# Attention scores of one head as three accumulating 32-row products in the four row quarters, with the shift as the exponential's bias

## What is computed

```python
q = (layernorm(x) @ Wq + bq).reshape(B, L, 16, 32)
k = (ctx @ Wk + bk).reshape(B, S, 16, 32)
v = (ctx @ Wv + bv).reshape(B, S, 16, 32)
scores = jnp.einsum('blhe,bshe->bhls', q, k)
A = jax.nn.softmax(scores / sqrt(32), axis=-1)
out = jnp.einsum('bhls,bshd->blhd', A, v)
x = x + out.reshape(B, L, 512) @ Wo + bo
x = x + routed_experts(layernorm(x))
```

## Time and profile before

| what | value |
|---|---|
| three runs | 2516.39, 2518.48, 2520.16 us |
| profiled execution, span from first to last instruction | 2509.0 us |
| profiled execution, its own time | not listed apart; the runs' median is 9.5 us above its span |
| TensorE, VectorE, ScalarE, GpSimd busy | 96%, 86%, 73%, 16% of the span |
| stages | projections to about 289 us, attention to about 2057, then output projection, routing, experts |

### The profile page before, as it was taken

The page is one execution under the profiler, slowest core; times in us unless marked ns, Lnnn a source line. Parts: engine busy times, 40 slices in busy tenths (PEclk is TensorE's granted clock), DMA queues, the critical chain, the costliest instruction groups (busy, mean ns, idle before and its releaser), DMA issues. The chain is left out here.

```text
span 2509.0 us, 36972 instructions
## 1 busy us (share of the span) xinstructions
PE 2419.7 (96%) x13522; PEld 1284.1 (51%) x13522; DVE 2152.2 (86%) x1941; ACT 1839.9 (73%) x2157; POOL 402.6 (16%) x512
## 2 busy tenths in 40 slices
PE   8999679999999999999999999999999999969998
PEld 7878434444444444444444444444444447758776
DVE  4368479999999999999999999999999998867555
ACT  3123368998988899899899988989889975634332
POOL 2113200100000000000000000000000003225665
PEclk9999789999999999999999999999999999979999
DMA  7436790011142001104100111510110107734473
GB/s 270 157 130 218 192 213 22 23 22 27 26 111 51 22 23 27 27 22 122 40 22 23 27 27 29 128 27 23 24 30 22 31 25 266 235 110 144 131 224 121
DMA packets 131353, 214.12 MB, mean 85 GB/s; under 512 B 26823, under 2 KB 64167, under 8 KB 130413
## 3 DMA queue, kind: packets, MB, share of 16 engines
q1 hardware_dynamic: 104268, 144.67, 20.7%
q0 software_dynamic: 24576, 59.52, 7.8%
q10 hardware_dynamic: 2336, 7.60, 0.9%
HBM read 146.36 MB, written 83.04 MB: 91 GB/s over the span
## 5 line engine op out<-in xcount | busy, mean ns | idle before, releaser
L1118 ACT ACTIVATE probs<-psum 128x1024 f32<-128x1024 f32 x1600 | 1508.9, 1035 | 149.8 <-PE psum L1269 145.7
L1269 PE MATMUL psum<-q_st,k_st 97*128 97x512 f32 x3200 | 922.9, 419 | 32.5 <-ACT probs L1118 17.5
L1269 PEld LDWEIGHTS psum<-q_st,k_st 97*128 97x128 f32 x3200 | 548.8, 189 | 609.7 <-ACT probs L1118 413.7
L1181 DVE TENSOR_TENSOR even_sums<-even_sums,probs 128x2048 f32<-128x2048 f32 x352 | 804.6, 2286 | 16.9 <-ACT probs L1118 16.9
L1290 PE MATMUL psum<-probs,v_st 128*32 128x512 f32 x6400 | 800.0, 601 | 0.0
L1181 DVE TENSOR_TENSOR odd_sums<-odd_sums,probs 128x2048 f32<-128x2048 f32 x320 | 731.4, 2285 | 1.0
L1290 PEld LDWEIGHTS psum<-probs,v_st 128*32 128x32 f32 x6400 | 152.3, 108 | 352.2 <-issue 263.9
L2050 PE MATMUL psum<-we_hi,wo 128*128 x624 | 216.7, 408 | 5.3 <-DVE wo L1941 3.1
L798 POOL DMA_DIRECT2D sum_scratch<-shared_rows x31 | 18.3, 590 | 1212.8 <-ACT shared_rows L1076 1212.8
L1882 ACT ACTIVATE shared_rows<-hold 128x512 f32<-128x512 f32 x78 | 63.6, 815 | 103.2 <-DMA hold<-token_rows,whole 62.9
L2050 PEld LDWEIGHTS psum<-we_hi,wo 128*128 128x128 f32 x624 | 118.1, 189 | 32.7 <-issue 7.5
(11 more groups left out here) (230 smaller groups left out, 2030.3 us busy)
## 6 DMA issues: line engine op xcount, KB each, us to landing
q_st<-qh_scratch SPq DMA_DIRECT2D x64, 256.0 KB
k_st<-kh_scratch SPq DMA_DIRECT2D x56, 192.0 KB, 3.8
token_rows<-rows SPq DMA_DIRECT2D x8, 1028.0 KB, 6.7
xn<-in_x SPq DMA_DIRECT2D x16, 512.0 KB, 6.8
qh_scratch<-o_hi SPq DMA_DIRECT2D x8, 1024.0 KB, 4.5
ql_scratch<-o_lo SPq DMA_DIRECT2D x8, 1024.0 KB, 7.6
q_st<-ql_scratch SPq DMA_DIRECT2D x32, 256.0 KB
token_rows<-in_x SPq DMA_DIRECT2D x1, 8192.0 KB, 38.9
```

Of the source, the lines that this page charges most:

```text
L1118: nc.scalar.activation(probs[:, p_slot(it, t), 2 * half:2 * half + 2, :], psum[:, 2 * slot:2 * slot + 2, :], ACT.Exp, scale=SCALE).then_in ...
L1181: nc.vector.tensor_tensor(into[:], a, probs[:, p_slot(it, t)], ALU.add).then_inc(added, 1)
L1269: mm = nc.tensor.matmul(psum[:, 2 * slot + h % 2, :], k_st[:, h, t * P:(t + 1) * P], q_st[b][:, h, :], start=True, stop=True)
```

## The change

- `k_st` and `q_st` hold each head's 32 rows once, in the head's own row quarter (rows 32h to 32h+31), with high and low parts beside each other. Keys and queries come in two transfers instead of three, each over all 128 partitions.
- A head's scores of a tile are three matmuls of 32 rows that accumulate in its PSUM bank. They are issued term by term, the four heads of a term in the four row quarters and in four banks.
- Both pairs of a tile are issued together behind one wait, two tiles ahead of the weighing (`AHEAD_TILES`); `LEAD` and `burst_end` go.
- The shift is no longer in the product: each exponential takes `neg_bound` as a per-partition bias. The spread over 128 rows, its copy, its store and its load go; the root is scaled, and the norms are turned and repeated by a matmul with the identity.
- For wide inputs (`unbounded`) the bias is 0 and a second unrolled program with a fourth product carries each query's shift; TensorE and SyncE branch to one of two programs.
- The rest pair has three products over 128 rows, in which each head's two keys lie in its own rows. Fills of one row of ones go; `shift_ones`, `rest_shift` and a part of each `q_st` are filled by VectorE.

```diff
-LEAD = 7
+AHEAD_TILES = 2
+SHIFT_PART = 2
+TERMS = ((0, 0), (0, 1), (1, 0))
...
-                sp.wait_ge(neg_rows_ready, 1)
-                sp.dma_start(shift_d.rearrange("g j (c n) -> (g j c) n", n=CH), neg_rows.bitcast(F32)).then_inc(shift_stored, 16)
-
-                sp.wait_ge(shift_stored, 16)
-                load_shift(sp, g, 0, 0, g["q_in"][0])
...
-                act.activation(bound[:], widest[:], ACT.Sqrt, scale=SLACK).then_inc(bound_ready, 1)
-                act.wait_ge(neg_spread, 1)
-                act.activation(neg_rows, psum[:, Q_SUM_BANK, :], ACT.Copy).then_inc(neg_rows_ready, 1)
+                act.activation(bound[:], widest[:], ACT.Sqrt, scale=SCALE ** 2 * SLACK).then_inc(bound_ready, 1)
...
-                pe.transpose(psum[0:1, K_SUM_BANK, 0:P], norms[:], ident[:]).then_inc(norms_turned, 1)
-                pe.wait_ge(neg_ready, 1)
-                pe.matmul(psum[:, Q_SUM_BANK, :], ones_row[:], neg_bound[:], start=True, stop=True).then_inc(neg_spread, 1)
+                pe.matmul(psum[:, K_SUM_BANK, 0:P], norms[:].to_broadcast([P, P]), ident[:], start=True, stop=True).then_inc(norms_turned, 1)
...
 def load_queries(sp, g, b, it, count):
-    for r, src in enumerate((g["qh_d"], g["ql_d"], g["qh_d"])):
-        sp.dma_start(g["q_st"][b][r * DH:(r + 1) * DH, :, :].bitcast(F32),
-                     src.rearrange("(h d) j l -> d h (j l)", d=DH)[:, :, ds(it * CH, CH)]).then_inc(count, 16)
+    for part, src in enumerate((g["qh_d"], g["ql_d"])):
+        sp.dma_start(g["q_st"][b][:, part, :].bitcast(F32), src.rearrange("p j l -> p (j l)")[:, ds(it * CH, CH)]).then_inc(count, 16)
...
-        k_st = sb("k_st", [SH + 1, HG, S], F32R)
-        q_st = [q[0:SH + 1] for q in g["q_st"]]
+        k_st = sb("k_st", [P, 2, S], F32R)
+        q_st = g["q_st"]
...
-            for r, src in enumerate((kh_d, kh_d, kl_d)):
-                sp.dma_start(k_st[r * DH:(r + 1) * DH, :, first:first + n].bitcast(F32),
-                             src[:, ds(j, 1), first:first + n].rearrange("(h d) o s -> d (h o) s", d=DH)).then_inc(count, 16)
+            for part, src in enumerate((kh_d, kl_d)):
+                sp.dma_start(k_st[:, part:part + 1, first:first + n].bitcast(F32), src[:, ds(j, 1), first:first + n]).then_inc(count, 16)
...
                         nc.scalar.activation(probs[:, p_slot(it, t), 2 * half:2 * half + 2, :],
-                                             psum[:, 2 * slot:2 * slot + 2, :], ACT.Exp, scale=SCALE).then_inc(exp_done, 1)
+                                             psum[:, 2 * slot:2 * slot + 2, :], ACT.Exp, bias=neg_bound[:], scale=SCALE).then_inc(exp_done, 1)
...
-                fill_rows(dve, (HG // 2, HG), filled)
+                dve.memset(shift_ones[:].bitcast(F32), 1.0).then_inc(filled, 1)
+                for b in range(2):
+                    dve.memset(q_st[b][:, SHIFT_PART, :].bitcast(F32), 0.0).then_inc(filled, 1)
+                dve.memset(rest_shift[:].bitcast(F32), 0.0).then_inc(filled, 1)
...
+                def products(bank, h, b, t, term, start, stop):
+
+                    part, of = TERMS[term]
+                    rows = slice(h * DH, (h + 1) * DH)
+                    return nc.tensor.matmul(psum[:, bank, :], k_st[rows, part, t * P:(t + 1) * P], q_st[b][rows, of, :], start=start, stop=stop)
+
+                def scores(it, t, shifted):
+
+                    b, n = it % 2, place(t, 0)
...
+                    if it * NP + n + 1 >= S_RING:
+                        pe.wait_ge(exp_done, it * NP + n + 2 - S_RING)
+                    for term in range(len(TERMS)):
+                        last = term == len(TERMS) - 1 and not shifted
+                        for h in range(HG):
+                            bank = 2 * ((n + h // 2) % S_RING) + h % 2
+                            mm = products(bank, h, b, t, term, term == 0, last)
+                            if last and h % 2:
+                                mm.then_inc(s_ready, 1)
...
+                def step(it, shifted):
+
+                    for t in range(NT):
+                        if it == 0 and t == 0:
+                            for u in range(AHEAD_TILES):
+                                ahead(0, u, shifted)
+                        ahead(it, t + AHEAD_TILES, shifted)
+                        if t == REST_AT:
+                            weigh_rest(it)
+                        weigh(it, t)
...
+                    for it in range(NIT):
+                        step(it, True)
+                with pe.Else():
+                    for it in range(NIT):
+                        step(it, False)
```

More of the change, by code:

```diff
@@ L936, in piece_end, with queries_in @@
             return S if n == K_PIECES - 1 else sum(pieces[n]) * P
-        def fill_rows(eng, heads, count):
-            for n, (a, m) in enumerate(pieces):
-                eng.memset(k_st[SH:SH + 1, heads[0]:heads[1], a * P:piece_end(n)].bitcast(F32), 1.0).then_inc(count, 1)
+        def queries_in(it, shifted):
+            per = 48 if shifted else 32
+            return per * (it // 2 + 1) - (16 if shifted and it % 2 == 0 else 0)
         with nc.Block() as block:
@@ L1011, in result @@
                     store_result(sp, results, j, c)
-                def step(it):
+                def step(it, shifted):
                     j, c = divmod(it, NC)
@@ L1056, in _ @@
+                with sp.Else():
+                    weighted(False)
                 sp.wait_ge(s_ready, NIT * NP)
@@ new lines, in rest_scores @@
+                def rest_scores(it, shifted):
+                    b, bank = it % 2, 2 * (REST_PAIR % S_RING)
+                    pe.wait_ge(exp_done, it * NP + REST_PAIR + 1 - S_RING)
+                    if it % NC == 0:
+                        pe.wait_ge(added, it * adds + REST_KEYS_AT + 1)
+                    for term, (part, of) in enumerate(TERMS):
+                        mm = nc.tensor.matmul(psum[0:REST_ROWS, bank, :], rest_k[:, part, 0:REST_ROWS], q_st[b][:, of, :],
+                                              start=term == 0, stop=term == len(TERMS) - 1 and not shifted)
+                    if shifted:
+                        mm = nc.tensor.matmul(psum[0:REST_ROWS, bank, :], rest_shift[:, 0:REST_ROWS], q_st[b][:, SHIFT_PART, :], start=False, stop=True)
@@ L1336, in step @@
                             sum_even(it - 1)
-                for it in range(NIT):
-                    step(it)
+                pe.wait_ge(filled, FILLS)
+                with pe.If(pe.value_load(unbounded[0:1, 0:1], min_val=0, max_val=1) == 1):
+                    with pe.Fori(0, NG) as j:
+                        with pe.Fori(0, NC) as c:
+                            it = j * NC + c
+                            pe.wait_ge(ma_k_in, (j + 1) * 32)
+                            pe.wait_ge(ma_q_in, (it + 1) * 32)
+                            k = 0
+                            for t in range(TPC):
+                                for h in range(HG):
+                                    rows = slice(h * DH, (h + 1) * DH)
+                                    for half in range(2):
+                                        if k >= 2:
+                                            pe.wait_ge(ma_max, it * (TPC * HG * 2) + (k - 1))
+                                        elif k == 0:
+                                            pe.wait_ge(ma_max, it * (TPC * HG * 2))
+                                        k += 1
+                                        for b in range(4 * half, min(4 * half + 4, -(-S // CH))):
+                                            w = min(CH, S - b * CH)
+                                            for term, (part, of) in enumerate(TERMS):
+                                                mm = pe.matmul(psum[:, b, 0:w], q_st[0][rows, of, t * P:(t + 1) * P],
+                                                               k_st[rows, part, b * CH:b * CH + w], start=term == 0, stop=term == len(TERMS) - 1)
+                                        mm.then_inc(ma_mm, 1)
+                    pe.wait_ge(ma_q_in, (NIT * 2 + 3) * 16)
+                    for it in range(NIT):
[3 more added lines that the diff above has]
+                        step(it, False)
                 pe.wait_ge(wo_lo_ready, 2)
```

245 lines of the change are left out of this document (103 added, 142 removed).

## The result

The changed kernel takes 2755.99 us (median) against 2517.55 us for the kernel before beside it: **1.0946 times as long, interval 1.0928 to 1.0963.** The direction was forecast; the size was not: 2593 us was the forecast, 2535 to 2705 its range. Of its four timed executions three lie between 2754.57 and 2756.49 us; one took 5458.58 us and stands outside the ratio.

The account below looks back on a forecast made before the run. PE's own work was taken as the bound, DVE 2 us behind. Profiled span 2509 + 87 (32 iterations, each 2.7 us longer) - 12 at the start = 2584 us; with 9.5 us from span to median, forecast 2593, range 2535 to 2705.

Parts of the forecast that it names:

- What bounds the kernel now: Attention in the kernel before: PE's own work takes 53.4 of 54.46 us an iteration, DVE needs 52.4.
- ACT's step of 1.00 us: From one exponential to the next on ACT: 0.91 us becomes 1.00, some 52 us an iteration with small copies, still hidden.
- A group of four row quarters at 0.23 us: Score matmuls on PE: four heads' 32-row matmuls side by side take 0.23 us a group, 0.89 us a tile's scores.
- dear groups: Rival for the score matmuls: groups of four cost 0.30 us each, ring 2.30 us, 2700 us in all; chance 0.15.
- serial weight loads: Rival for the score matmuls: twelve weight loads follow one another, ring 2.63 us, 2971 us in all; chance 0.09.
- The ring of 2.16 us a tile: Exponential and scores wait for each other with nothing in reserve: 0.05 + 0.96 + 0.03 + 1.12 = 2.16 us a tile.
- The bias at 0.09 us: Per-partition bias on each exponential on ACT: 0.09 us longer, 1.03 to 1.12 us.
- The start at -12 us: Start of attention: first key load 3.3 us earlier and 9.0 us from less data ahead of Wo, together -12 us.
- The copy of O sits in the first of these gaps and costs nothing: In the sum for an iteration: ACT's copy of O falls in the gap at the first sum over keys, costing nothing.
- The clock rival: Rival for PE's clock: it falls to half, 120 us more for every tenth of the iterations; chance 0.04.
- The chance of 0.87 for slower: Whole kernel: slower by over 0.2% (5 us) was given 0.87, within that 0.04, faster 0.09.
- The signs: Trace marks of being right: rest-pair exponentials 57 us apart, exponentials near 1.12 us, DVE near 91%, Wo's split near 318 us.

Follow-up runs that it names:

- grain_f3: Kernel before, 97-row products and no bias, with both pairs of a tile behind one wait, two tiles ahead, and O copied before the fourth exponential: 2565.59 us, 1.0192.
- before_bias: Kernel before with a per-partition bias of zero added to every exponential of attention: 2571.58 us, 1.0222.
- fetch3_swap: fetch3 with the two waits ahead of a tile's scores exchanged, exponential first, then key piece: 2599.22 us, 1.0329.
- fetch3: Changed kernel with the copy of O moved from before the seventh exponential of an iteration to before the fourth: 2614.14 us, 1.0398.
- fetch3_nobias: fetch3 with the bias of the exponentials left out, so the shift is not applied: 2544.53 us, 1.0118.
- rows_pairs: Changed kernel with scores issued pair by pair, each with its own wait, in the old bursts: 2644.69 us, 1.0513.
- fetch5: Changed kernel with the copy of O one exponential earlier, before the sixth: 2699.72 us, 1.0735.
- grain_f6: grain_f3 with the copy of O back before the seventh exponential: 2669.72 us, 1.0627.
- wide_forced: Changed kernel with the test for wide inputs made to fail and the search loops unrolled: 8216.92 us, measured once.

## Why the prediction was right and wrong

- **What bounds the kernel now: right for PE, incomplete for ACT.** PE's own work was put at 53.4 us with DVE behind it; grain_f3 was summed from the same rows and came out within 0.3 us. But before_bias shows that ACT had no room to spare: 0.09 us more on each exponential made an iteration 1.69 us longer, where I had expected 1.0 at most, and where the prediction called ACT's step of 1.00 us "still hidden".
- **A group of four row quarters at 0.23 us: right.** The twelve matmuls and the switch take 0.90 us (985.72 - 984.82 in fetch3_swap), 0.89 was summed; they start in three groups of four, 0.33 and 0.23 us apart, the four of a group within 0.02 us. The way there was in part luck: the row it was read from shows a group of four side by side every 0.43 us in the weighing (four under way from 989.96, the next four from 990.41), and that such a matmul is two passes of 0.215 was assumed, not read. By the figure of 3.07 times in the Trainium skill (TensorE: Matmul & The Clock Gate, Measured speedup vs the span model), which I had held against the row, a group would cost an estimated 0.30 and these scores 1.03 us; the trace does not agree with it for this kernel. The rivals of dear groups and of serial weight loads fall with the same rows; the second was also summed too high, since its 1.43 and an exponential of 1.12 make a ring of 2.55 and not 2.63.
- **The ring of 2.16 us a tile: right**, 2.17 in the trace. In the unhindered form, fetch3_swap, an iteration is 57.59 us for 57.2 summed. Missed here: 0.10 us where a tile has two waits, 0.6 us an iteration. The remaining 0.4 was not traced.
- **The bias at 0.09 us: right**, 1.024 to 1.113 us, and in the ring with its full length.
- **The start at -12 us: right** in sum. Wo's split began at 319.07 us instead of 330.24, 11.2 us earlier (forecast near 318). The single terms shifted: SP's jump over the long program cost more than my 1.5 us. In the trace SP's branch ends at 285.23 and the first key load goes out 2.85 us later, at 288.08; in the kernel before these were 290.03 and 290.15. So the first key load is 2.1 us earlier, not 3.3, and less data ahead of Wo gave the rest:

```profile
284.35 1.28 ACT L1052 ACT_TABLE_LOAD   x1 [4.34 <-PEq L252]
...
288.08 0.33 SPq L889 DMA_DIRECT2D k_st<-kh_scratch  x1
...
319.07 1.91 ACT L1081 ACTIVATE wo<-even_sums 128x2048 fp32r<-128x2048 f32 x1 [2.35 <-DMA even_sums<-in_Wo]
```

- **The step that failed** stands in the list of an iteration: "The copy of O sits in the first of these gaps and costs nothing". I had asked what the copy does to ACT, and not who waits for it. The weighing of tile 0 does, and in the new order the scores of tile 3 are queued behind it. Put at nothing, it costs 4.38 us an iteration, 141.85 us in all (2755.99 - 2614.14 us), of which about two thirds are the wait and one third the slow clock. With that term the forecast of 2593 becomes 2735; most of the 21 us still missing is the order of the two waits (14.9 us between fetch3 and fetch3_swap).
- **The clock rival** had 0.04 on the ground that "the gaps here are under 0.5 us". That was about true of tiles (at most 0.53 us in fetch3, whose clock stays at 1.00). Behind the gap of 2.78 us that I had missed, the clock comes down in 24 of 30 iterations, for about 1.5 us an iteration, some 46 us in all.
- The chance of 0.87 for slower rested on the ring and holds: with the missed wait removed the kernel is still slower, by 3.98%. Of that, fetch3_nobias takes the bias (2.25 us an iteration) and grain_f3 the order (1.59); the row quarters themselves give back 0.12.
- **The signs** that were named: exponentials near 1.12 us and the wait of each tile's first weight load are there. Rest-pair exponentials are 62.6 us apart instead of 57 and DVE is busy 85% instead of 91%, both mostly through the missed wait.

## What to carry to other kernels

When an order of issue is made shorter (fewer pieces in hand, coarser steps behind one wait), go through every wait in the queue of the engine that issues them, not only the one that was edited: a consumer that had been far behind now stands right ahead of the producer, and a release that was placed for the old distance is late. Where two engines feed each other through a small ring, add the full latencies around it, semaphore to semaphore, before counting busy time; anything put into it, such as a bias operand of 0.09 us, is paid in full each time around. And relief for the bounding engine is worth only the distance to the next bound: here 0.23 us a tile less work on TensorE brought 0.12 us an iteration.

## What the runs showed of the hardware

- Four 32-row matmuls of 512 columns in four row quarters and four banks run at the pace of one, 0.23 us from group to group in fetch3_swap, with ScalarE reading PSUM beside them.
- Matmuls in other row quarters need not be issued together, and do not start in the order of the program: in rows_pairs the first matmul of a pair started 0.02 us after the first of the pair before it, although five matmuls stand between the two in the program, and four of them started 0.34 and 0.57 us after that first one.
- Which wait comes first in the program matters: the scores of tiles with two waits started 0.10 us later behind the exponential, and not after the two were exchanged.
- A jump over a long program can cost time: SyncE's first transfer came 2.85 us after its branch in the changed kernel, 0.12 us after it in the kernel before.
- In fetch5 TensorE stood still for 1.79 us once an iteration, and in 17 of 30 iterations the granted clock fell from 2.4 to 1.2 GHz, beginning between 0.3 us before and 0.7 us after work resumed; with 2.16 us (grain_f6) it fell in 20 of 30, with 2.78 us (the changed kernel) in 24. In fetch3, whose longest idle time in attention is 0.53 us, it stayed at 1.00.
- In the search of wide_forced, TensorE was busy 323.72 of 400 us with 862 matmuls of 32 rows, 21 at a time one after another in one row quarter (0.43 us from start to start at 512 columns), and was granted 0.50 from 1000 to 1400 us, that is 1.2 GHz. The groups in four quarters that alternate with weighings were granted 0.98 in the same execution.
